# First z of a batched hypergraph block: the order of its statistics, drains and splits, and GpSimd's additions beside them

## The reference

```python
h = jnp.maximum(_layernorm(x, axis=-1), 0.0)
x = x + _L0_gnn_ref(h, adj, W1, b1, gamma, beta, W2, b2)

def hypergraph_conv(x, adj, W, b):
    H = (adj != 0).astype(x.dtype)
    w = adj.reshape(N, -1)[:, :C]                 # the first row of adj
    xw = jnp.einsum('ncd,hd->nch', x, W)
    Dn = 1 / einsum('nce,ne->nc', H, w)           # 0 where the sum is 0
    Be = 1 / H.sum(axis=1)                        # 0 where the sum is 0
    m = Be[:, :, None] * jnp.einsum('nce,nch->neh', H, xw)
    out = Dn[:, :, None] * jnp.einsum('nce,neh->nch', H, m)
    return out + b

def _L0_gnn_ref(x, ...):
    h = jax.nn.relu(hypergraph_conv(x, adj, W1, b1))
    h = layer_norm(h, gamma, beta)
    y = hypergraph_conv(h, adj, W2, b2)
    return y + x
```

## Time and profile before

| | |
|---|---|
| time, median of 3 runs | 640.25 us (639.63 to 640.46) |
| the profiled execution's own time | 639.93 us |
| its span, first to last instruction | 638.1 us |
| granted TensorE clock | 1.00 in every stretch |
| busy PE | 619.6 us, 97% of the span |
| busy DVE | 475.1 us, 74% |
| busy ACT | 290.3 us, 45% |
| busy POOL | 110.9 us, 17% |
| PE waits on line 563 for the transposes of z | 3.5 us in 3 waits |

### The profile page before, as it was taken

The page is one execution under the profiler, slowest core; times in us unless marked ns, Lnnn a source line. Parts: engine busy times, 40 slices in busy tenths (PEclk is TensorE's granted clock), DMA queues, the critical chain, the costliest instruction groups (busy, mean ns, idle before and its releaser), DMA issues.

```text
span 638.1 us, 11993 instructions
## 1 busy us (share of the span) xinstructions
PE 619.6 (97%) x4808; PEld 467.1 (73%) x4808; DVE 475.1 (74%) x1148; ACT 290.3 (45%) x540; POOL 110.9 (17%) x132
## 2 busy tenths in 40 slices
PE   2999799999999999999999999999999999999998
PEld 1756658688586885778766886768858688586887
DVE  6899878976689765995779948798478876388632
ACT  4464935373435635364353632646335373125620
POOL 0114019422210304004040040401212012000000
PEclk9999999999999999999999999999999999999999
DMA  8995680169810696108951099213990159000701
GB/s 336 257 349 106 124 339 2 33 126 187 348 34 2 151 222 288 34 1 201 250 211 34 22 225 299 116 34 82 203 357 21 34 115 207 10 1 2 196 3 67
DMA packets 146215, 89.78 MB, mean 141 GB/s; under 512 B 134896, under 2 KB 135536, under 8 KB 141168
## 3 DMA queue, kind: packets, MB, share of 16 engines
q1 hardware_dynamic: 146160, 89.02, 51.6%
HBM read 47.06 MB, written 8.39 MB: 87 GB/s over the span
## 4 chain that ended last, share of the span: by engine, by line
PE 92%; DVE 4%; ACT 2%; DMA 1%; issue 0%
PE acc L582 18%; PE acc L599 18%; PE acc L522 15%; PE acc L563 12%; PE acc L543 11%; PE acc L502 7%; PE acc L504 7%; PE acc L484 2%; PE acc L443 1%; PE acc L445 1%; DVE z L937 1%; DMA z<-z_split_ring 1%; ACT z_split_ring L671 1%; ACT z L672 1%; DMA x_in<-x 1%; DVE incidence L873 1%
## 5 line engine op out<-in xcount | busy, mean ns | idle before, releaser
L582 PE MATMUL acc<-xw_split,incidence 128*128 128x256 f16 x1024 | 113.2, 273 | 0.0
L599 PE MATMUL acc<-edge_means,incidence_t 128*128 128x256 f16 x1024 | 113.1, 273 | 0.0
L582 PEld LDWEIGHTS acc<-xw_split,incidence 128*128 128x128 bf16 x1024 | 100.1, 98 | 13.2 <-DVE xw_split L973 0.2
L599 PEld LDWEIGHTS acc<-edge_means,incidence_t 128*128 128x128 bf16 x1024 | 100.2, 98 | 13.1
L629 ACT ACTIVATE edge_means<-acc,edge_inverse 128x256 f16<-128x256 f32 x128 | 55.2, 472 | 116.1 <-PE acc L582 68.4
L502 PE MATMUL acc<-h_split,incidence 128*128 128x257 f16 x448 | 98.6, 273 | 0.0
L504 PE MATMUL acc<-h_split,incidence 128*128 128x256 f16 x448 | 98.6, 273 | 0.0
L522 PE MATMUL acc<-incidence_t,edge_means 128*128 128x512 bf16 x448 | 97.8, 379 | 0.0
L563 PE MATMUL acc<-w_split,z 128*128 128x256 f16 x768 | 85.5, 273 | 3.5 <-DMA z<-z_split_ring 3.5
L563 PEld LDWEIGHTS acc<-w_split,z 128*128 128x128 f16 x768 | 74.9, 98 | 13.1 <-DVE edge_means L1024 2.7
L543 PE MATMUL acc<-w_split,pt_split 128*128 128x512 f16 x384 | 84.2, 379 | 0.0
(11 more groups left out here) (104 smaller groups left out, 639.4 us busy)
## 6 DMA issues: line engine op xcount, KB each, us to landing
adj_in<-adj SPq DMA_DIRECT2D x32, 1024.0 KB, 10.2
out<-residual SPq DMA_DIRECT2D x32, 256.0 KB, 2.6
x_in<-x SPq DMA_DIRECT2D x7, 1024.0 KB, 5.5
edge_weights<-adj SPq DMA_DIRECT2D x7, 512.0 KB, 3.7
x_in<-x SPq DMA_DIRECT2D x2, 512.0 KB, 4.6
z<-w1t SPq DMA_DIRECT2D x1, 512.0 KB, 12.5
xw_split<-w2t SPq DMA_DIRECT2D x1, 512.0 KB, 13.2
incidence_t<-incidence SPq DMA_TRANSPOSE x32, 4.8
```

What stands on the lines that cost most here:

```text
L582: last = nc.tensor.matmul(acc[:, 0:DOUT], inc[:, b.slot, ct, P * et:P * (et + 1)], xw[:, ct, part, :], start=(ct == 0 and part == HI), sto ...
L599: last = nc.tensor.matmul(acc[:, 0:DOUT], inc_t[:, b.slot, ct, et, :], edge[:, et, part, :], start=(et == 0 and part == HI), stop=(et == T ...
```

## The change

On DVE the statistics of z's tiles 2 and 3 and the whole variance of the lower half move ahead of the drains of tiles 4 to 7, and the inverse root of the lower half stands behind the drain of tile 4. In the upper half, `z_lo` of tiles 0, 1 and 2 and `edge_inverse(nxt, 0)` move forward: `z_lo(0)` ahead of the last statistics, `z_lo(1)` ahead of the upper variance, `z_lo(2)` and `edge_inverse` ahead of the upper inverse root.

On ACT the square root of the lower half comes two ReLU tiles earlier, and the splits of tiles 0, 1 and 2 stand between the ReLUs of tiles 4 to 7. The square root of the upper half now stands behind the split of tile 2.

On GpSimd the W2 subtraction goes first; it waits for all of batch 1's incidence (`inc_ready`, 16) besides `w_hi`. The eight additions come after it and wait for the end of the lower chain (`z_half`, 11) instead of for the fourth drain.

```diff
--- before.py
+++ after.py
@@ -407,11 +407,12 @@
             pool.wait_ge(w_hi, 1)
             pool.wait_ge(x_step, 2 * X_STEPS)
             nc.gpsimd.tensor_tensor(w1s[:, :, LO, :], w1f, w1s[:, :, HI, :], ALU.subtract).then_inc(w_ready, 1)
-            pool.wait_ge(c_drained, T // 2)
+            pool.wait_ge(inc_ready, 2 * T)
+            pool.wait_ge(w_hi, 2)
+            nc.gpsimd.tensor_tensor(w2s[:, :, LO, :], gf, w2s[:, :, HI, :], ALU.subtract).then_inc(w_ready, 1)
+            pool.wait_ge(z_half, Z_STEPS)
             for t in range(T):
                 nc.gpsimd.tensor_tensor(res[:, 1, t, :], x_in[:, t, :], res[:, 1, t, :], ALU.add).then_inc(x_added, 1)
-            pool.wait_ge(w_hi, 2)
-            nc.gpsimd.tensor_tensor(w2s[:, :, LO, :], gf, w2s[:, :, HI, :], ALU.subtract).then_inc(w_ready, 1)
             pool.wait_ge(x_added, 2 * T)
             add_h0(Batch(0, 2))
             pool.wait_ge(b2_loaded, 16)
@@ -778,17 +779,19 @@
             copy(w2s[:, :, HI, :], gf, scale=wr[:, 3:4])
             z_relu_tile(b0, 1)
             copy(gf, gf, scale=wr[:, 3:4]).then_inc(w_hi, 1)
-            for t in range(2, T // 2 + 1):
-                z_relu_tile(b0, t)
+            z_relu_tile(b0, 2)
+            z_relu_tile(b0, 3)
             act.wait_ge(z_half, 4)
             nc.scalar.activation(z_ln[:, 1, 0:T // 2], z_ln[:, 0, 0:T // 2], ACT.Sqrt).then_inc(z_half, 1)
-            for t in range(T // 2 + 1, T):
-                z_relu_tile(b0, t)
+            z_relu_tile(b0, 4)
             z_split(b0, 0)
+            z_relu_tile(b0, 5)
+            z_relu_tile(b0, 6)
             z_split(b0, 1)
+            z_relu_tile(b0, 7)
+            z_split(b0, 2)
             act.wait_ge(z_step, 4)
             nc.scalar.activation(z_ln[:, 1, T // 2:T], z_ln[:, 0, T // 2:T], ACT.Sqrt).then_inc(z_step, 1)
-            z_split(b0, 2)
             z_split(b0, 3)
             t1_hi_part(b1_, 0)
             t1_hi_part(b1_, 1)
@@ -1134,24 +1137,24 @@
             drain_c(b0, 3)
             z_stats(b0, 0)
             z_stats(b0, 1)
+            z_stats(b0, 2)
+            z_stats(b0, 3)
+            variance(z_ln, z_stat, z_half, b0, Z_STEPS, DH, lower)
             drain_c(b0, 4)
-            z_stats(b0, 2)
+            inverse_root(z_ln, z_half, b0, Z_STEPS, ZN_SCALE, lower)
             drain_c(b0, 5)
-            z_stats(b0, 3)
             drain_c(b0, 6)
-            variance(z_ln, z_stat, z_half, b0, Z_STEPS, DH, lower)
+            z_stats(b0, 4)
             drain_c(b0, 7)
-            z_stats(b0, 4)
-            inverse_root(z_ln, z_half, b0, Z_STEPS, ZN_SCALE, lower)
             z_stats(b0, 5)
             z_stats(b0, 6)
+            z_lo(b0, 0)
             z_stats(b0, 7)
+            z_lo(b0, 1)
             variance(z_ln, z_stat, z_step, b0, Z_STEPS, DH, upper)
-            z_lo(b0, 0)
-            z_lo(b0, 1)
+            z_lo(b0, 2)
+            edge_inverse(nxt, 0)
             inverse_root(z_ln, z_step, b0, Z_STEPS, ZN_SCALE, upper)
-            edge_inverse(nxt, 0)
-            z_lo(b0, 2)
             z_lo(b0, 3)
             t1_lo_part(nxt, 0)
             t1_lo_part(nxt, 1)
```

## The result

The changed kernel takes 638.0 us (median of 18 runs, 636.67 to 640.57); the kernel before, measured beside it, 640.15 (638.97 to 642.33). The ratio is 0.9971, 95% interval 0.996 to 0.9982: faster by 0.3%, 1.9 us by the ratio and 2.15 by the medians, where 2.2 was forecast.

A forecast was written before the change was run, and what follows sets the result against it. PE bounds, waiting in stage D of batch 0 for transposes of z. Earlier transposes end D at 82.35 instead of 84.52, gain 2.2 us: 640.25 − 2.2 = 638.05 us, 8-in-10 range 636.7 to 639.2.

The forecast's parts named there:

- what bounds: PE in stage D of batch 0: waits three times for transposes of z, about 4.2 us open.
- the lower chain: DVE, lower half of z: ends at 57.9, where the first split began at 63.53; first split gains 5.6 us.
- the collision: DVE beside GpSimd's moved additions: first low parts and upper variance wait 0.6, 0.1 and 0.7 us, 1.4 in all.
- the packets' price: Stage D: instruction packets in flight lengthen z's second and third transposes by 0.8 and 1.5 us.
- the place: PE's packet tied to D's third tile, at 75.2 in the third transpose's flight; DVE's at 70.2 in the second's.
- I take both prices again: Stage D: second transpose again lands 4.5 us after issue, third 5.3, each with a packet in flight.
- the prediction's own signs: Traces of stage D: among the listed signs, a fourth transpose taking over 5 us means rival 2.
- rival 2: Stage D: packets hit the fourth transpose as well; D ends at 83.2, gain 1.3 us, time 638.95; chance 0.14.
- 3, the lock takes it back: DVE's five two-SBUF-input operations each lose to a GpSimd addition; slower, 641 to 641.7 us; chance 0.04.
- 4: Lower chain meets another port holder, costing up to 2.1 us; chance 0.08, shared with gains otherwise given back.
- 1, no packet in the way: Stage D: no packet in the third transpose's flight; gain 2.8 to 3.5 us, time 637.4 to 636.8; chance 0.29.

The follow-up runs named there:

- Third profile: The unaltered changed kernel run once more for another profile; 636.76 us (1 run).
- second profile: The unaltered changed kernel measured and profiled again on the second chip; 638.15 us, ratio to the kernel before 0.9969.
- e2_order_only: Kernel before with only the change's DVE and ACT parts, GpSimd's program as before; 641.52 us, ratio 1.0015.
- e5_after_58: Changed kernel with 58 one-element dummy matmuls at PE's start, shifting its instruction packets; 636.68 us, ratio to the kernel before 0.9938.
- e7: Kernel before with 58 one-element dummy matmuls at PE's start; 639.28 us, ratio 0.9982.
- e1: Kernel before with only GpSimd's part of the change; 638.95 us, ratio 0.9979.
- e9_warm_58: Changed kernel with 58 wide dummy matmuls (128 by 128 times 128 by 224) at PE's start; 636.73 us, ratio to the kernel before 0.9942.

## Why the prediction was right or wrong

**Right: what bounds.** The gain lies in stage D of batch 0 alone. What follows D is 553.5 or 553.6 us long in all three traces (the earlier trace rows and above).

**Right: the lower chain.** With the drain of tile 3 0.82 us earlier than in the trace of before (51.99 for 52.81), the first split should begin at 57.1; it began at 57.15. The W2 subtraction lay at 51.41 to 53.54, beside the end of a drain and statistics alone, and held nothing up. (On ACT the square root of the lower half moved ahead of one ReLU, that of tile 4, and not of two.)

**Right in kind, too high in size: the collision.** `z_lo(0)` was to wait 0.6 us, `z_lo(1)` 0.1, the upper variance 0.7: 1.4 in all. Measured: 0.46, 0 and 0.51, together 0.97. GpSimd did go ahead of the variance, as assumed; it only had less of its addition left. The transposes were issued at 67.10, 70.48 and 74.03, which on the prediction's time are 67.9, 71.3 and 74.85, 0.3 to 0.4 us before the forecast 68.3, 71.65 and 75.2.

**Right: the packets' price. Wrong in part: the place.** "I take both prices again" held: 4.3 and 5.2 or 5.3 us for the forecast 4.5 and 5.3. But I tied PE's packet to a fixed distance behind the start of D's third tile and put it on the third transpose. That is one of two places. Third profile: D's third pair began 6.83 us after D, forecast 7.25, and D took 12.18, forecast 12.5. Its one wait, 1.43 us before D's fifth tile, is the forecast's 1.6. First and second profile: the packet fell on the fourth. By the prediction's own signs (a fourth that takes over 5 us) that is rival 2, which had a chance of 0.14, though that had the second, third and fourth late; here the third was on time, so without the half clock D would have taken 13.0.

**Not foreseen: the half clock.** A gap in front of the last pair costs twice, 2.2 us of wait and 1.7 us of slow matmuls. By the three profiles the packet's place decides between the two, and with it which group a run belongs to. A third of the runs have nearly no gain, the rest have some 2.4 us (their median is 637.75). The median of all runs falls at the upper end of the quick group, so that 638.05 and 638.0 agree to 0.05 us is luck: the forecast knew nothing of the slow third. The kernel before has slow runs too (8 of 25 on the first chip at 640.95 or more, seven of them with a clock of 0.997 or less); none of them has a profile.

**Rivals.** 3, the lock takes it back, came about only in `e2_order_only`, where GpSimd keeps its old order and holds up the lower chain; in the changed kernel it had two additions left at that point, as assumed. 4 did not occur. 1, no packet in the way, is `e5_after_58`: forecast 637.4 to 636.8, measured 636.68, just under it. The Trainium skill (Runtime: NRT & Kernel Launch, section "Instruction fetch mechanics"), which I named there, calls the crossing of a block mostly hidden. At this place of the program it isn't: `e5` and `e7` show that moving the packet away is worth 1 to 1.5 us, and the rows show PE waiting for the transfer that the packet falls in. What the packets cost elsewhere no run here tests.

**Left out by the argument.** I called additions of two SBUF inputs the ones that wait. `e1` and `e2` show four-column operations with one SBUF input waiting as well (0.65 us for a `tensor_scalar` that takes 0.17 alone). And the variance has five operations with two SBUF inputs, not three: its square and its `scalar_tensor_tensor` read two as well, and the latter took 0.58 us for 0.16 in both kernels. In the changed kernel none of these others had an addition beside it, so it cost the forecast nothing.

## What to carry to other kernels

Where one engine's small dependent operations stand in the critical chain, look at what the neighbour on the same SBUF ports runs at that moment, and move that first: here GpSimd's order alone was worth 1.3 us in the medians, the chain's order alone nothing or less. When a transfer on the critical path lands late now and then, look for a packet of the instruction queue in its flight before blaming the transfer, and count a wait of PE as possibly more than its length, since the clock may fall behind it. Profile a changed kernel more than once when its runs fall in two groups, and set each profile's own time beside the median: one trace can show none of the gain.

## What the runs showed of the hardware that I had not expected

- A DMA transpose with PE's instruction packet (q8) 1 us or more behind its issue landed 5.1 to 5.8 us after it instead of 3.6 to 3.8 (ten transposes); 4.0 and 4.2 where the packet came within 0.6 us; with q14's packet 4.2 to 4.6.
- PE's granted clock fell to half for 3.4 us behind waits of 2.2, 2.4 and, twice, 2.7 us (once of these at the start of the program, in `e9_warm_58`), and did not behind waits of 1.4, 2.0, 2.2 and, once, 2.4.
- At the start of the program, behind the same 11.6 us of idle time, the matmuls' pace doubled between 14.3 and 16.9 us, while the granted clock read 1.00 throughout.
- Four-column `tensor_scalar` operations on DVE with one SBUF input waited for GpSimd's additions (0.65 to 0.66 us for 0.17), while drains from PSUM and statistics of 512 columns did not.
